# Opening stage of a graph and expert layer: x normalised in place, four buffers of part rows, transfers in multiples of 16 rows, roots of two groups at once

## What is computed

```
edge_index = stack([src, dst])
x = x + gnn(layernorm(x), edge_index, gnn_weight, gnn_bias)
x = x + ffn(layernorm(x)[None], gate_w, gate_b, w1, b1, w2, b2)[0]

gnn:  agg = segment_sum(x[src], dst) / max(deg, 1)
      out = concat([x, agg]) @ weight;  out = out / norm(out) + bias
ffn:  idx = argmax(softmax(x @ gate_w + gate_b));  prb = its probability
      pos = place of the row among the rows of its expert;  kept = pos < C
      y = (relu(x @ w1[idx] + b1[idx]) @ w2[idx] + b2[idx]) * prb * kept
```

## Time and profile before

| what | value |
|---|---|
| time, median of 3 runs (lowest, highest) | 1463.89 us (1462.98, 1465.42) |
| time of the profiled execution | 1461.04 us |
| its span, first to last instruction | 1459.3 us |
| busy: TensorE, VectorE, ScalarE, GpSimd | 75%, 60%, 34%, 63% |
| mean granted TensorE clock | 0.94 |
| first gather issued | 111.30 us |
| HBM read, written | 207.46 MB, 39.29 MB |

### The profile page before, as it was taken

The page is one execution under the profiler, slowest core; times in us unless marked ns, Lnnn a source line. Parts: engine busy times, 40 slices in busy tenths (PEclk is TensorE's granted clock), DMA queues, the critical chain, the costliest instruction groups (busy, mean ns, idle before and its releaser), DMA issues.

```text
span 1459.3 us, 33188 instructions
## 1 busy us (share of the span) xinstructions
PE 1101.7 (75%) x6813; PEld 797.5 (55%) x6814; DVE 874.6 (60%) x3786; ACT 495.6 (34%) x1397; POOL 923.8 (63%) x946
## 2 busy tenths in 40 slices
PE   0105667668888888888889889888888888876885
PEld 0004445446666666666666666666666666654553
DVE  2973545446666676666667666666756675654443
ACT  1651111223333333333333333333333333343442
POOL 3446676757777777777777777777776777600101
PEclk9998777879999999999999999999999999998998
DMA  7257888865565656566565655656564656411111
GB/s 210 89 185 211 299 267 287 286 213 162 163 179 165 183 162 186 168 174 179 155 176 149 181 159 168 168 160 174 149 179 131 176 152 174 127 38 43 37 48 35
DMA packets 126952, 238.78 MB, mean 164 GB/s; under 512 B 21453, under 2 KB 85250, under 8 KB 126932
## 3 DMA queue, kind: packets, MB, share of 16 engines
q0 software_dynamic: 55904, 160.90, 38.6%
q1 hardware_dynamic: 71028, 77.69, 16.9%
HBM read 207.46 MB, written 39.29 MB: 169 GB/s over the span
## 4 chain that ended last, share of the span: by engine, by line
DVE 25%; DVEq 20%; PE 20%; issue 17%; DMA 14%; ACT 3%; SPq 1%; ACTq 1%; POOL 1%; POOLq 0%
PE ps_q L726 7%; DVEq L1300 5%; PE ps_h L793 4%; DMA ring<-parts_d,idx 4%; PE ps_a L784 4%; DVE sel L1049 3%; DVEq L1120 3%; DMA b_b<-in_L_ffn_b 2%; DMA parts_d<-w_sb 2%; DVEq L903 2%; DVE row L1163 2%; DMA out<-ys,node_i 2%; DMA w_sb<-in_x 2%; DVE row L1167 1%; DVE acc L1058 1%
## 5 line engine op out<-in xcount | busy, mean ns | idle before, releaser
L476 POOL DMA_INDIRECT ring<-parts_d,idx x784 | 768.2, 980 | 278.5 <-issue 184.4
L726 PE MATMUL ps_q<-ring,sel 128*128 128x256 bf16 x2928 | 474.6, 287 | 165.8 <-DVE sel L1049 90.4
L726 PEld LDWEIGHTS ps_q<-ring,sel 128*128 128x128 bf16 x2928 | 255.1, 102 | 325.0 <-issue 205.4
L1049 DVE SCALAR_TENSOR_TENSOR sel<-lane,block,dst_t 128x512 bf16<-128x512 bf16 x245 | 184.1, 751 | 121.2 <-PE ps_q L732 63.2
L812 PE MATMUL ps_b<-w_sb,hid_t 128*128 x864 | 231.0, 397 | 23.7 <-ACT hid_t L646 23.7
L793 PE MATMUL ps_h<-w_sb,hid_t 128*128 x432 | 211.1, 615 | 5.7 <-ACT hid_t L625 5.7
L1058 DVE TENSOR_TENSOR acc<-acc,ps_q 128x257 f32 x245 | 103.2, 421 | 164.0 <-ACT cat L600 68.1
L812 PEld LDWEIGHTS ps_b<-w_sb,hid_t 128*128 128x128 f32 x864 | 150.1, 190 | 48.3 <-issue 33.7
L732 PE MATMUL ps_q<-ones_bf,sel 128*128 128x1 bf16 x976 | 167.3, 171 | 0.0
L784 PE MATMUL ps_a<-gw_sb,cat_t 128*128 128x256 f32 x416 | 127.6, 435 | 0.9 <-ACT cat_t L622 0.9
L646 ACT ACTIVATE hid_t<-ps_t,b_t 128x128 f32<-128x128 f32 x432 | 117.6, 383 | 30.5 <-PE ps_t L801 30.5
(11 more groups left out here) (189 smaller groups left out, 1307.2 us busy)
## 6 DMA issues: line engine op xcount, KB each, us to landing
w_sb<-in_L_ffn_w SPq DMA_DIRECT2D x32, 512.0 KB
ring<-parts_d,idx POOLq DMA_INDIRECT x784
disp_d<-ys SPq DMA_DIRECT2D x8, 1040.0 KB, 12.9
parts_d<-w_sb SPq DMA_DIRECT2D x6, 1344.0 KB, 5.1
xs<-disp_d SPq DMA_DIRECT2D x55, 130.0 KB, 3.2
ys<-disp_d SPq DMA_DIRECT2D x55, 130.0 KB
b_b<-in_L_ffn_b SPq DMA_DIRECT2D x55, 128.0 KB
xb<-in_x SPq DMA_DIRECT2D x51, 128.0 KB
```

The lines of the kernel that those rows point to most:

```text
L476: pool.indirect_dma_start(ring[:, (k % 2) * TQ + j, :], None, parts_d[:, :], bass.IndirectOffsetOnAxis(ap=idx[:, k * TQ + j:k * TQ + j + 1 ...
L726: mm = pe.matmul(ps[:, 0:D], sel[:, s, j, :], ring[:, (k % 2) * TQ + j, part * D:(part + 1) * D], start=(j == 0 and part == 0), stop=(j == ...
L1049: dve.scalar_tensor_tensor(out=sel[:, s, :, :], in0=lane[:, :].rearrange("p (j m) -> p j m", j=1).to_broadcast((P, TQ, P)), scalar=block0[ ...
```

## The change

- x is staged in seven buffers, one for each group, all in the space of w1; there are no `xn`, `r1` and `dst_m` any more. Normalised values overwrite x, and the remainder overwrites those. So `rest(g)` waits for ScalarE's copy of the top half (`hi_copied`).
- `parts` has NPB = 4 buffers.
- `rstds` and `rstd_start` treat two groups at once (the last one alone). Epsilon is added in the logarithm's bias and in the Newton step; the row L992 is gone.
- Loads and stores of 97 rows become 96 and 1, those of 106 become 96 and 10; group 0 of x is loaded in four blocks and three.
- VectorE clears the ends of the edge lists and all of `acc`, ahead of everything else. GpSimd no longer clears `acc`; its casts of the edge lists stand ahead of the constants' loads. VectorE forms the last group's low part (`last_low`).
- ScalarE's copies of the transposed edge lists stand before its work on group 0, from two PSUM tiles in turn.
- `edge_lists` follows `stats(0)`, `quad_table` stands in group 0; the clamp to the last node is made on the four minima and maxima.
- SyncE: the filler row is stored first and comes from `hid`; w2 is issued directly behind w1, ahead of the wait for finished rows; the first loads of a chunk (`load_xs`, `load_ys`) stand ahead of the loop; the wait for the fill moves to ScalarE.

The diff, cut to its core:

```diff
-        xin = [carve(w1_flat, s * XW, XW) for s in (0, 1, 6, 8)]
-        xn = [carve(w1_flat, (2 + s) * XW, XW) for s in range(2)]
-        r1 = [carve(w1_flat, (4 + s) * XW, XW) for s in range(2)]
-        parts = [carve(w2_flat, s * NPART * XW // 2, NPART * XW // 2).bitcast(BF16) for s in range(2)]
+        xin = [carve(w1_flat, g * XW, XW) for g in range(NG)]
+        parts = [carve(w1_flat, NG * XW, PW).bitcast(BF16)]
+        parts += [carve(w2_flat, s * PW, PW).bitcast(BF16) for s in range(NPB - 1)]
...
+                pieces = ((0, 4), (4, XG)) if g == 0 else ((0, blocks),)
...
+                    for lo, hi in ((0, LASTA), (LASTA, LAST)):
+                        sp.dma_start(parts_d[(NB - 1) * P + lo:(NB - 1) * P + hi, :],
+                                     parts[s][lo:hi, (XG - 1) * NPART * D:XG * NPART * D]).then_inc(parts_out[s], 16)
...
-                sp.dma_start(staged[0:FULLQ - QH, QE:2 * QE],
-                             dram[QH * QE:FULLQ * QE].rearrange("(p e) -> p e", e=QE)).then_inc(stage_in, 16)
+                sp.dma_start(staged[0:ROWSA, QE:2 * QE],
+                             dram[QH * QE:(QH + ROWSA) * QE].rearrange("(p e) -> p e", e=QE)).then_inc(stage_in, 16)
...
                     load_weights(t, 0)
+                    load_weights(t, 1)
...
-                if weights:
-                    load_weights(t, 1)
...
+            load_xs(C0)
+            load_ys(C0 - 1)
             with sp.Fori(0, C0) as t:
                 trip(t, chunk=False, weights=True)
-            sp.wait_ge(fill_out, 16 * C0)
-            load_xs(C0)
-            load_ys(C0 - 1)
...
-                pool.memset(acc[:, g * AC:(g + 1) * AC], 0.0)
...
+            rstd_start(0, 2)
+            for m, to in enumerate((dst_t, src_t)):
+                for h, ps in enumerate((ps_a, ps_t)):
+                    act.wait_ge(edges_t, 2 * m + h + 1)
+                    act.activation(to[:, h * QH:(h + 1) * QH, :].rearrange("p q j -> p j q"),
+                                   ps[:, 0:TQ, 0:QH], ACT.Copy).then_inc(edges_copied, 1)
...
+                if g % 2 and g + 1 < NG:
+                    rstd_start(g + 1, min(2, NG - g - 1))
...
             def rest(g):
-                dve.wait_ge(xn_act, g + 1)
-                if g >= 2:
-                    dve.wait_ge(mid_copied, g - 1)
-                    dve.wait_ge(low_done, g - 1)
-                dve.tensor_tensor(r1[s][:, :], xn[s][:, :],
-                                  xn[s][:, :].bitcast(BF16).rearrange("p (d t) -> p d t", t=2)[:, :, 1],
+                dve.wait_ge(hi_copied, g + 1)
+                dve.tensor_tensor(xin[g][:, :], xin[g][:, :],
+                                  xin[g][:, :].bitcast(BF16).rearrange("p (d t) -> p d t", t=2)[:, :, 1],
                                   ALU.subtract).then_inc(r1_ready, 1)
...
+            dve.memset(dst_i[ROWSA:QH, QE:2 * QE], PAD_DST)
+            dve.memset(src_i[ROWSA:QH, QE:2 * QE], 0).then_inc(stage_clear, 1)
+            dve.memset(acc[:, :], 0.0)
             stats(0)
+            edge_lists()
             stats(1)
+            rstds(0, 2)
             for g in range(NG):
-                rstds(g)
+                normal(g)
                 if g:
                     rest(g - 1)
                 if g + 2 < NG:
                     stats(g + 2)
-                if g == 1:
-                    edge_lists()
-                if g == 4:
+                if g % 2 and g + 1 < NG:
+                    rstds(g + 1, min(2, NG - g - 1))
+                if g == 0:
                     quad_table()
             rest(NG - 1)
+            dve.drain()
+            last_low()
```

More of the change, by code:

```diff
@@ L30 @@
 XA = 5
+NPB = 4
+LASTA = LAST // 16 * 16
+ROWSA = (FULLQ - QH) // 16 * 16
 NG = NB // XG
@@ L85, in gnn_moe_layer @@
         rev9 = sb("rev9", [P, EX], FP32)
+        eps_t = sb("eps_t", [P, 1], FP32)
         off1 = sb("off1", [P, NB], FP32)
@@ L172, in gnn_moe_layer @@
         xn_dve = sem("xn_dve")
+        acc_clear = sem("acc_clear")
+        filler = sem("filler")
         xn_act = sem("xn_act")
@@ L179, in gnn_moe_layer @@
         low_done = sem("low_done")
-        parts_out = [sem(f"parts_out{s}") for s in range(2)]
+        parts_out = [sem(f"parts_out{s}") for s in range(NPB)]
         stage_f = sem("stage_f")
@@ L243, in chunks, with parts_stored @@
             return t - (C0 - 1)
+        def parts_stored(s, upto):
+            return 16 * sum(3 if g == NG - 1 else 1 for g in range(s, upto, NPB))
         @block.sync
@@ L414, in _ @@
             pool.memset(ones[:, :], 1.0)
+            pool.memset(eps_t[:, :], EPS)
+            pool.memset(ones_bf[:, :], 1.0).then_inc(pool_step, 1)
+            pool.wait_ge(pool_step, 1)
+            pool.affine_select(out=ident[:, :], in_=ident[:, :], compare_op=ALU.not_equal, fill=1.0,
+                               base=0, pattern=[[-1, P]], channel_multiplier=1)
+            pool.affine_select(out=tri[:, :], in_=tri[:, :], compare_op=ALU.is_ge, fill=0.0,
+                               base=0, pattern=[[1, P]], channel_multiplier=-1).then_inc(consts, 1)
             pool.memset(seen[:, :], 0.0)
@@ L423, in _ @@
             pool.memset(row[:, :], 0.0)
-            pool.memset(ys[:, 0:C_NODE], 0.0)
-            pool.memset(ys[:, C_NODE:C_NODE + 1], float(FAR))
+            pool.memset(hid[:, 0:C_NODE], 0.0)
+            pool.memset(hid[:, C_NODE:C_NODE + 1], float(FAR)).then_inc(filler, 1)
             pool.memset(xb[:, :], 0.0)
-            pool.memset(ones_bf[:, :], 1.0).then_inc(pool_step, 1)
             pool.iota(lane[:, :], [[1, P]], base=0, channel_multiplier=0, allow_small_or_imprecise_dtypes=True)
@@ L533, in _, with rsqrt_start @@
         def _(act):
-            def rsqrt_start(to, of, tmp):
-                act.activation(tmp, of, ACT.Ln)
+            def rsqrt_start(to, of, tmp, plus=0.0):
+                act.activation(tmp, of, ACT.Ln, bias=plus)
                 act.drain()
@@ L540, in _, with rstd_start @@
             act.wait_ge(consts, 1)
-            def rstd_start(g):
-                o = (g % 2) * 2 * XG
-                act.wait_ge(var1_ready, g + 1)
-                rsqrt_start(nt1[:, o + XG:o + 2 * XG], mv1[:, o + 1:o + 2 * XG:2], nt1[:, o:o + XG]
+            def rstd_start(first, groups):
+                lo, hi = first * XG, (first + groups) * XG
+                act.wait_ge(var1_ready, first + groups)
+                rsqrt_start(nt1[:, lo:hi], mv1[:, 2 * lo + 1:2 * hi:2], ln1[:, lo:hi], eps_t[:, :]
                             ).then_inc(ln1_ready, 1)
             def parts_view(g):
-                return parts[g % 2][:, :].rearrange("p (b k d) -> p b k d", k=NPART, d=D)
+                return parts[g % NPB][:, :].rearrange("p (b k d) -> p b k d", k=NPART, d=D)
             def top_half(f32):
@@ L659, in _ @@
                 trip(t, chunk=False)
+            act.wait_ge(fill_out, 16 * C0)
             with act.Fori(C0, TRIPS) as t:
@@ L686, in _ @@
             for m, staged in enumerate((dst_f, src_f)):
-                for h in range(2):
-                    if m or h:
-                        pe.wait_ge(edges_copied, 2 * m + h)
+                for h, ps in enumerate((ps_a, ps_t)):
+                    if m:
+                        pe.wait_ge(edges_copied, h + 1)
                     for j in range(TQ):
-                        last = pe.transpose(ps_a[:, j, 0:QH], staged[0:QH, h * QE + j * P:h * QE + (j + 1) * P],
+                        last = pe.transpose(ps[:, j, 0:QH], staged[0:QH, h * QE + j * P:h * QE + (j + 1) * P],
                                             ident[0:QH, 0:QH])
@@ L982, in stats @@
             def stats(g):
-                o = (g % 2) * 2 * XG
-                dve.wait_ge(xin_in[g], 16 * (1 if g < NG - 1 else 2))
                 x_g = xin[g][:, :].rearrange("p (b d) -> p b d", d=D)
+                o = g * 2 * XG
                 for b in range(XG):
+                    if b == 0:
+                        dve.wait_ge(xin_in[g], 16 * (1 if g < NG - 1 else 3))
+                    elif g == 0 and b == 4:
+                        dve.wait_ge(xin_rest, 16)
                     dve.bn_stats(bn1[:, b * 6:(b + 1) * 6], x_g[:, b, :])
```

187 lines of the change are left out of this document (84 added, 103 removed).

## The result

The changed kernel takes 1441.73 us (median of 4 runs, 1440.05 to 1445.04) against 1463.43 us for the kernel before beside it (1457.35 to 1465.42): a ratio of 0.9859, 95% interval 0.9833 to 0.9884. It is faster by 21.7 us, 1.4%. Forecast were 1434 us, 1425 to 1446, and a saving of 29.5. A later set of runs on one chip gave 1446.51 against 1463.46 us, ratio 0.9877 (0.9846 to 0.9907), a saving of 17.0.

What follows compares the result with a forecast made beforehand. GpSimd's gather stream was taken to set the pace through all 49 trips. Opening 24, less 1.5 for the first burst, plus 7 for the hole gave 29.5 us saved: 1434 us, range 1425 to 1446.

Steps and rivals of the forecast that it cites:

- Opening: Stretch before the gather stream: earlier first gather and TensorE visits save 24 us, bounds 18.6 to 27.6.
- first burst: First weight loads of the loop: they grow by 1 MB, shared with gathers, costing 1.5 us, between 0 and 3.7.
- The lock: Opening, group 6: VectorE's remainder waits out GpSimd's subtraction for group 5; without this the sum is 1.7 us shorter.
- Edge loads: Opening, rival at 4%: the 98-row pieces stay slow, VectorE waits 7 us at the edge lists, 1441 us.
- main case: Whole kernel: the forecast as summed holds, 1426 to 1443 us, at 68%.
- The lock by the big memset: Opening, rival at 10%: GpSimd's small rows and VectorE's acc memset exclude each other, slide of 5 to 8 us, 1439 to 1443.
- Hole: Ahead of trip 8: TensorE and GpSimd no longer stand waiting for the last expert weights, 7 us saved, from 4 to 7.5.
- The step that failed: Trips 1 to 7: issuing both expert halves together leaves the mixture of transfers unchanged, so nothing is lost there.
- I am wrong if the loading trips grow: Sign against the forecast: loading trips should stay at 23 to 24 us before and after.
- slower: Loading trips, rival at 2%: larger early bursts displace gathers, 5 us a trip, 40 in all, 1474 us.

Runs made afterwards that it cites:

- w2 late: Changed kernel with the second half of an expert's weights again issued behind the wait for finished rows: 1443.21 us, ratio 0.9860.
- last pair: Changed kernel again, 1446.51 us, beside the same kernel with only the loading trips' order altered to second half, fill, first half, 1436.63 us.
- w2 first: Changed kernel with loading trips issuing second half, fill, first half, all ahead of the wait for finished rows: 1436.63 us, ratio 0.9807.

## Why the prediction was right, and where it was off

- **Opening, forecast 24.** Measured 23.85 at the first finished rows. This mark includes the first burst, for which the forecast took off 1.5, so 22.5 was due there. The 24 was chosen between 23.4 for the second visit and 25.9 for the first gather; they came 22.9 (99.64 against 122.58) and 26.5 us sooner, the first visit 22.2 against 20.0. On the way: the memset of `acc` 10.55 us (11.8 from the row of 512, bounds 10.4 and 13.1), but from 4.77 on, 3 us later than I had it, after 2.69 us of idleness that the profile puts down to nothing; roots' end near 26.8 against 25.1, those of groups 4 and 5 at 54.5 against 54.6, tables 77.85 against 78.6, first gather 84.80 against 85.4, first visit 92.84 against 95.1. The upper bound of the opening was added up wrongly: 25.9 and 1.4 for the shorter memset are 27.3, not 27.6. The memset's 0.84 ns an element lies near the slope between two rows that I had kept as the lower bound. One cycle for an element, by the Trainium skill's "VectorE: DVE Perf Modes", section on zero memsets, gave 13.1 as an estimate; this row doesn't agree, by 2.5 us.
- **The lock.** The last remainder started at 72.48 beside GpSimd's subtraction (to 73.85) and took 3.25 instead of 2.02: the block is there, 1.2 us of it, where I had 1.7 to 2.
- **Edge loads.** Quick, as in the main case. The lock by the big memset was a rival at 10%; GpSimd's rows beside it kept their lengths, and casts ran at 11.04.
- **Hole, forecast 7.** Measured 8.0 in trip 8 (31.7 to 23.7), and 6.4 by the pair with w2 late and first (29.7 and 23.3).
- **The step that failed:** "In trips 1 to 7 nothing changes in the mixture: second half, fill and first half already left within 6 us of one another." The mixture is the same, the order is not. By the order rows of SyncE in the change itself, w2 came ahead of the next trip's fill before and behind it after; I looked at how close they leave and not at which goes first. The term measures -9.7 us, 1.4 a trip (-10.7 between the orders of the last pair), where I had 0; my -1.5 was for the first burst alone, which lies ahead of them. "I am wrong if the loading trips grow" stood among the signs, and they grew, from 23.5 to 24.9 us. The rival "slower" had this mechanism, bursts that displace gathers in each loading trip, priced at 5 us a trip and 2%; the mechanism was real at a quarter of its price, far from the 3.7 at which it would decide.
- **The sum.** 23.85 - 9.7 + 8.0 = 22.1, measured 21.7 and 17.0 by medians. The time fell into the stated range because that range, 21 us wide, has room for a whole term that is missing, and because the opening and the hole gave 2.4 more than forecast. Opening and hole were right; trips 1 to 7, put at nothing, were not. With w2 first the changed kernel saves 26.8 of the forecast 29.5. Between 22.1 and 17.0 lies what is still open: the stretch behind trip 8 takes 1128.3 to 1135.4 us in the five traces of changed kernels on such chips, against 1125.2 in the one trace of before. Whether the change costs later trips a few microseconds, or that execution was a quick one, the runs don't settle.

## What to carry to other kernels

When a transfer is moved, write down the order of the burst on both sides of the move, and who waits for each piece. Here two exchanged lines were worth 9.9 us, more than the 8.0 of the hole that the move had removed, and without them the move gained nothing. The same exchange cost 6.6 us on a chip with slower trips, so such an order is to be measured on the chips that count. A piece that seems to be wanted late, like the fill, may have a waiter in every trip. Give a long clearing to the engine that idles at that moment, and not to one beside whose run the small rows of the engine that everyone waits for stand still.

## What was not expected of the hardware

- Chips differ: the same kernel before takes 1463 us on some and 1733 on others. The traces of the slower ones show nearly the same opening and later trips of about 29.5 us instead of 23.4. The sign of an effect can differ with them (w2 first against the changed kernel: -9.9 us on the quicker kind, +6.6 on the other).
- A VectorE row of 14 columns can last 10.27 us beside a run of GpSimd memsets, while rows with two inputs pass in 0.17.
- ScalarE clears 12593 elements a partition in 11.25 us, VectorE in 10.55 and GpSimd in 10.87: what decides among them is who idles at that moment, and whom the clearing holds up.
